# First level's steps at their own distances in chain slots, third norm of the isolated rows beside the fourth level, 31 dense slots beside the second level

## The reference

```
x = layernorm(x + L0(x))   # two-layer MLP, then a degree-normalised sum over edges and self loops
x = layernorm(x + L1(x))   # graph convolution with edge weights, relu, graph convolution
x = layernorm(x + L2(x))   # attention: leaky relu, z = h W, softmax of scores over the edges of a dst
x = layernorm(x + L3(x))   # messages from both ends and edge features, summed at dst, update MLP
# layernorm: (x - mean) / sqrt(var + 1e-5), no scale, no shift
```

## Time and profile before

| what | value |
|---|---|
| median of 3 runs (all) | 2968.99 us (2963.08, 2968.99, 2969.27) |
| profiled execution: own time, span | 2964.16 us, 2962.4 us |
| busy, share of the span: POOL, PE, DVE, ACT | 73%, 73%, 67%, 48% |
| mean granted TensorE clock | 0.852 |
| chain that ended last | POOL 54%, issue 20%, DVE 11%, PE 9%, DMA 3% |
| of it by line | POOL g_row L860 38%, x_with_info 8%, out_rows 7% |

### The profile page before, as it was taken

One profiled execution on the slowest core, in us unless ns is written; L12 is line 12 of the kernel. 1 busy time (PEld: TensorE's weight loads), 2 busy tenths in 40 slices (PEclk: granted clock), 3 DMA queues, 4 the chain that ended last, 5 costly groups with the idle time before them and its releaser, 6 DMA issues.

```text
span 2962.4 us, 39045 instructions
## 1 busy us (share of the span) xinstructions
PE 2167.5 (73%) x10332; PEld 1145.4 (39%) x10332; DVE 1987.5 (67%) x3848; ACT 1436.1 (48%) x2755; POOL 2174.0 (73%) x1666
## 2 busy tenths in 40 slices
PE   3998999959878646766577768998355576666665
PEld 1444444434444323434344434444255333333332
DVE  5665688858888747788599985777599433333332
ACT  2876677746545335565345446676222232233232
POOL 7888877778887258888588858888333688888887
PEclk9999999979989868897799979999655687777777
DMA  7998522223666366767354443443387322222221
GB/s 212 277 280 232 140 58 59 56 55 82 138 136 133 93 132 153 164 150 164 84 115 115 114 100 84 99 109 80 80 189 187 84 57 55 56 56 57 56 50 25
DMA packets 624034, 338.13 MB, mean 114 GB/s; under 512 B 536607, under 2 KB 585101, under 8 KB 623818
## 3 DMA queue, kind: packets, MB, share of 16 engines
q1 hardware_dynamic: 550217, 288.96, 38.8%
q0 software_dynamic: 73600, 46.68, 9.3%
HBM read 203.61 MB, written 130.80 MB: 113 GB/s over the span
## 4 chain that ended last, share of the span: by engine, by line
POOL 54%; issue 20%; DVE 11%; PE 9%; DMA 3%; SPq 2%; ACT 1%; DVEq 0%; POOLq 0%; ACTq 0%
POOL g_row L860 38%; POOL x_with_info L867 8%; POOL out_rows L867 7%; PE bank L1078 2%; PE bank L1101 2%; DVE rT L1696 1%; PE pair L987 1%; DMA g_row<-t_x,gidx 1%; DVE agg L1718 1%; PE bank L987 1%; PE pair L1058 1%; DVE x_r L1673 1%; DVE agg L1776 1%; DVE ss L1619 1%; PE pair L1069 1%
## 5 line engine op out<-in xcount | busy, mean ns | idle before, releaser
L860 POOL DMA_INDIRECT g_row<-t_x,gidx x600 | 814.0, 1357 | 263.6 <-issue 218.9
L1288 ACT ACTIVATE hid<-pair,b_up 128x1000 f32<-128x1000 f32 x375 | 406.1, 1083 | 45.9 <-PE pair L1059 44.2
L1079 PE MATMUL bank<-hid,w_dn 128*64 128x500 f32 x750 | 423.6, 648 | 0.0
L1078 PE MATMUL bank<-hid,w_dn 128*64 128x500 f32 x750 | 423.6, 648 | 0.0
L860 POOL DMA_INDIRECT g_row<-x_with_info,src_i x200 | 275.4, 1377 | 69.3 <-issue 56.7
L1058 PE MATMUL pair<-xT,w_top 64*128 64x500 f32 x550 | 314.6, 653 | 13.0 <-ACT hid L1288 10.5
L860 POOL DMA_INDIRECT g_row<-t_h,gidx x200 | 260.4, 1302 | 81.1 <-issue 80.8
L1059 PE MATMUL pair<-xT,w_bot 64*128 64x500 f32 x550 | 315.0, 654 | 0.0
L860 POOL DMA_INDIRECT g_row<-in_x,dst_i x200 | 260.2, 1301 | 68.0 <-issue 67.6
L1269 ACT ACTIVATE xT<-bank 128x500 f32<-128x500 f32 x275 | 160.3, 583 | 280.2 <-DVE rT L1696 163.2
L867 POOL DMA_INDIRECT out_rows<-n_r,fidx x200 | 251.2, 1256 | 60.9 <-issue 60.6
(11 more groups left out here) (257 smaller groups left out, 5157.9 us busy)
## 6 DMA issues: line engine op xcount, KB each, us to landing
x_in<-in_x_cols SPq DMA_DIRECT2D x100, 250.0 KB, 3.2
x_with_info<-wide SPq DMA_DIRECT2D x50, 476.0 KB
wide<-in_x SPq DMA_DIRECT2D x50, 448.0 KB
out_rows<-x_r SPq DMA_DIRECT2D x100, 224.0 KB
l_k<-keep_row SPq DMA_DIRECT2D x150, 125.0 KB
l_a<-t_x SPq DMA_DIRECT2D x150, 112.0 KB
l_k<-on_row SPq DMA_DIRECT2D x50, 250.0 KB
t_x<-x_r SPq DMA_DIRECT2D x100, 112.0 KB
```

The costliest lines, as they stand in the source:

```text
L860: return g.indirect_dma_start(out=to, out_offset=None, in_=table, in_offset=bass.IndirectOffsetOnAxis(ap=index[:, tile:tile + 1], axis=0), ...
L1078: T.matmul(run.down[0:D, 0:CH], w_dn[a.stage][:, 0:D], hid[a.b2][:, 0, :], start=True, stop=True)
L1079: T.matmul(run.down[D:128, 0:CH], w_dn[a.stage][:, 0:D], hid[a.b2][:, 1, :], start=True, stop=True)\
L1288: A.activation(hid[a.b2][:, :, :], run.up[a.b2][:, :, 0:CH], ACT.Relu, bias=b_up[:, a.stage:a.stage + 1]).then_inc(Cn["hid"], 1)
```

## The change

The steps of stage A are no longer hung on the arrival of the next isolated blocks. Each has its own distance, in chain slots, from the place of its block: `agg` 2 as before, `aggT` 3, `t1`, `t2` and `sq` 4, `ssum`, `std` and SP's load 5, `rows` 6, SP's store 7. No dense blocks stand among the isolated ones any more (`DENSE_MIXED` 3 to 0), and level B gets 31 places instead of 22. `third` moves as a whole from level B to level D, with its store one turn later and three more calls on SP after D's turns; the waits for its stores move with it, on DVE from the end of B to the end of D, ahead of the memsets.

```diff
-DENSE_MIXED = 3
-BESIDE_B, BESIDE_D, BESIDE_G = 22, 74, 0
+DENSE_MIXED = 0
+BESIDE_B, BESIDE_D, BESIDE_G = 31, 74, 0
...
-        def blocks_due(n):
-            return [a.b for a in ISO if a.place[0] + 2 == n] + [NI + i for i in range(5) if ISO[-1].place[0] + 3 + i == n]
-        def behind(b, lag):
-            b -= lag
-            return (b, b % 2, b % 4) if 0 <= b < NI else None
+        def block_at(n, slots):
+            found = [a.b for a in ISO if a.place[0] + slots == n]
+            return (found[0], found[0] % 2, found[0] % 4) if found else None
...
-            for step, at in (("rows", 4), ("st", 4), ("ld", 1), ("y", 0), ("sq", 1), ("ssum", 2), ("std", 3)):
+            for step, at in (("rows", 4), ("st", 5), ("ld", 1), ("y", 0), ("sq", 1), ("ssum", 2), ("std", 3)):
...
             with_a = sp_chain(WITH_A)
             for n in SLOTS_A:
-                for b in blocks_due(n):
-                    slot_a(b)
+                if c := block_at(n, 5):
+                    if c[0] + 4 < NI:
+                        ld_a(c[0] + 4)
+                if c := block_at(n, 7):
+                    st_a(c[0])
                 with_a(n)
...
 (SP, levels B and D)
-                  also=(...), each=third, run=WITH_B)
+                  also=(...), run=WITH_B)
-                  D_ld, [LD["lky2"]], D_st, LD["zc"], ..., behind=2, run=WITH_D, late=1)
+                  D_ld, [LD["lky2"]], D_st, LD["zc"], ..., behind=2, run=WITH_D, late=1, each=third)
+            for k in range(NC + 2, NC + 5):
+                third(k)
...
+            for r in range(2):
+                sp.wait_ge(third_st[r], 32 * len(range(r, NI, 2)))
...
 (PE)          aggT:  behind(b, 1)  ->  block_at(n, 3), after with_a(n)
 (ACT)         std:   behind(b, 3)  ->  block_at(n, 5);  sq: behind(b, 2) -> block_at(n, 4)
 (DVE, slot_a, between first(n) and rest(n), in this order)
               rstd:  behind(b, 4)  ->  block_at(n, 6)
               t1:    behind(b, 2)  ->  block_at(n, 4)
               ssum:  behind(b, 3)  ->  block_at(n, 5)
               rows:  behind(b, 4)  ->  block_at(n, 6)
               t2:    behind(b, 2)  ->  block_at(n, 4)
               agg:   behind(b, 0)  ->  block_at(n, 2)
...
 (ACT and DVE) each=third leaves shared_slots of WITH_B and joins that of WITH_D
-            shared_slots(slot_b, rest, WITH_B, 4, before=first, each=third)
-            for r in range(2):
-                dve.wait_ge([F["st0"], F["st1"]][r], 32 * len(range(r, NI, 2)))
+            shared_slots(slot_b, rest, WITH_B, 4, before=first)
...
-            shared_slots(slot_d, rest, WITH_D, 4, before=first)
+            shared_slots(slot_d, rest, WITH_D, 4, before=first, each=third)
+            for r in range(2):
+                dve.wait_ge([F["st0"], F["st1"]][r], 32 * len(range(r, NI, 2)))
```

More of the change, by code:

```diff
@@ L767, in _ @@
                   B_ld, [LB["xb"]], B_st, LB["rows"], lambda k, q: (rows_of(t2_d)[k], v4(n_r[q][:, :])), behind=3,
-                  also=(B_bst, LB["base"], lambda k, q: (chunks(base_d)[k], v4(l_src[q][:, :]))), each=third, run=WITH_B)
+                  also=(B_bst, LB["base"], lambda k, q: (chunks(base_d)[k], v4(l_src[q][:, :]))), run=WITH_B)
             all_stored(sp, B_st)
@@ L778, in _ @@
             level(lambda k, q: [(half(l_a[q]), rows_of(t3_d)[k])],
-                  D_ld, [LD["lky2"]], D_st, LD["zc"], lambda k, q: (z_d[k], zx[q % 2][:, :]), behind=2, run=WITH_D, late=1)
+                  D_ld, [LD["lky2"]], D_st, LD["zc"], lambda k, q: (z_d[k], zx[q % 2][:, :]), behind=2, run=WITH_D, late=1, each=third)
+            for k in range(NC + 2, NC + 5):
+                third(k)
             for r in range(2):
@@ L1104, in _ @@
             pe.wait_ge(Cn["rows"], normed_before(MAIN.hi))
-            def slot_a(b):
-                if c := behind(b, 1):
+            with_a = chain(WITH_A)
+            for n in SLOTS_A:
+                with_a(n)
+                if c := block_at(n, 3):
                     k, p, q = c
@@ L1114, in slot_a @@
                     mm.then_inc(LA["aggT"].sem, 1)
-            with_a = chain(WITH_A)
-            for n in SLOTS_A:
-                with_a(n)
-                for b in blocks_due(n):
-                    slot_a(b)
             pe.wait_ge(Cn["rows"], normed_before(WITH_A.hi))
@@ L1315, in _ @@
             HT2 = pair[1][:, 0, :]
-            def slot_a(b):
-                if c := behind(b, 3):
+            with_a = chain(WITH_A)
+            for n in SLOTS_A:
+                with_a(n)
+                if c := block_at(n, 5):
                     k, p, q = c
@@ L1322, in slot_a @@
                     root(a_sd[:, :], a_ss[:, :]).then_inc(LA["std"].sem, 1)
-                if c := behind(b, 2):
+                if c := block_at(n, 4):
                     k, p, q = c
@@ L1379, in _ @@
             act.wait_ge(s_idx, I_ALL)
-            shared_slots(slot_b, chain(WITH_B), WITH_B, 4, each=third)
+            shared_slots(slot_b, chain(WITH_B), WITH_B, 4)
             def after_c(at):
@@ L1410, in _ @@
             at_least(act, LC["rows"], NC)
-            shared_slots(slot_d, chain(WITH_D), WITH_D, 4)
+            shared_slots(slot_d, chain(WITH_D), WITH_D, 4, each=third)
             act.wait_ge(LD["c"], D_EXP)
@@ L1736, in block_scalar, with slot_a @@
                 return col.rearrange("p (s k) -> p s k", s=2).unsqueeze(3).to_broadcast([R, 2, TC, D])
-            def slot_a(b):
-                if c := behind(b, 4):
+            def slot_a(n):
+                if c := block_at(n, 6):
                     k, p, q = c
@@ L1767, in slot_a @@
                     V.tensor_tensor(a_w[p][:, :], a_v[:, :], a_base[q], ALU.add).then_inc(LA["t2"].sem, 1)
-                if c := behind(b, 0):
+                if c := block_at(n, 2):
                     k, p, q = c
@@ L1784, in _ @@
                 first(n)
-                for b in blocks_due(n):
-                    slot_a(b)
+                slot_a(n)
                 rest(n)
```

5 lines of the change are left out of this document (removed).

## The result

The changed kernel takes 2942.75 us (median of 4 runs, 2938.16 to 2945.02) against 2966.03 of the kernel before on the same chip (4 runs, 2960.08 to 2969.27): a ratio of 0.9916 with an interval of 0.9893 to 0.9939. The sign was right, the size was not.

The account below looks back on a forecast made before the run. POOL's gathers were taken to bound every stage touched. A -14, B -1, C 0, D +5 and D's end +3 gave -7 on the profiled 2964.16 us, so 2957, or 2959 with all four runs as one sample; range 2946 to 2972.

Parts of the forecast that it names:

- the third norm's part in B's slow gathers: Stage B: the third norm's leaving quickens the gathers by 4 us, within bounds of 0 to 23.
- a later last chunk: End of B: the chain runs until the last turns, so DVE may reach the last chunk later, +3 us (0 to 7).
- The `info` wait: Stage A: one POOL wait of 5.47 us instead of 0.30, for a late `info`, goes; last gather ends at 971.7.
- SP's lateness: Stage A: slow store issues make DVE wait 1 to 2 us in one pair of three; 3 us charged (0 to 20).
- The 4 us of slower gathers: Stage D: the third norm's instructions slow the gathers by 4 us (0 to 23), part of D's +5.
- End of D: +3: End of D: DVE's memsets wait for the last third-norm store, +2.8 us (1 to 5).
- Rival 1: A -17, B -8 + 3, D 0 to +1, end +3: -18 in all, 2948 us; chance 0.17.
- Rival 2: Stage D: third-norm instructions delay DVE, each of 25 double turns loses 0.5 us more; +5, 2971 us; chance 0.10.
- rival 3: Stage A: stores land 2 us late in every pair, 19 us of lateness instead of 3; +9, 2975 us; chance 0.11.
- Rival 4: Gathers stop for the full length of third-norm two-input instructions: B -20, D +36; +5 in all, 2971 us; chance 0.04.
- Seven instructions of 0.6 us: A's tail: DVE work that leaves the slots before SP's store waits, 4.4 us off the 66.7 from block 24's relu to B.
- the chances of the same time and of a slower one: Whole kernel: same within about 0.2% given 0.34, slower 0.15, faster 0.51, summed from forecast and rivals.

Follow-up runs that it names:

- e1: Changed kernel with three mixed dense blocks, 22 places beside B and the third norm in B as before, so own distances alone: 2952.23 us, ratio 0.9938.
- g3: Kernel before, with SP leaving a dense block's columns for a later slot instead of standing in a wait for them: 2944.41 us, ratio 0.992.
- e2: Kernel before, with only the third norm moved from B to D: 2956.89 us, ratio 0.9953.
- f1: Changed kernel with the old places (three mixed dense blocks, 22 places beside B); distances and third norm in D stay: 2937.8 us, ratio 0.9896.
- g2: g1 with the old places (three mixed dense blocks, 22 places beside B): 2917.33 us, ratio 0.9822.
- f4: Changed kernel, with SP leaving a dense block's columns for a later slot instead of standing in a wait for them: 2919.63 us, ratio 0.9836.
- f5: Changed kernel with the third norm's steps in D closer together, for its last store two turns earlier: 2937.33 us, ratio 0.9899.
- g1: Changed kernel with the changes of both f4 and f5: 2916.96 us, ratio 0.9833.
- h1: e2 plus 75 unused two-input VectorE instructions (125x512, both inputs in SBUF) in B: 2997.9 us, one run.
- h2: e2 plus 75 unused VectorE reductions of 125x512 from SBUF in B: 2961.9 us, one run.
- h4: e2 plus 75 unused VectorE float32 copies of 125x512, SBUF to SBUF, in B: 2972.94 us, one run.
- h3: Kernel before plus the 75 unused two-input VectorE instructions of h1, but in D: 2965.64 us, one run.
- e3: Kernel before with only the new places (no mixed dense blocks, 31 places beside B), third norm still in B: 2999.94 us, ratio 1.0099.
- e4: Changed kernel with the third norm left in B, so new places and own distances: 2993.24 us, ratio 1.0072.

## Why the prediction was wrong

It gave -7 us against a measured -26 of the two profiled executions; the 19 between lie as follows.

**B: the step that failed** is the price of the third norm's leaving. The prediction said of the third norm's part in B's slow gathers: "By its share of B's DVE work, 51.6 of 260.1 us, it is 4.6; I take 4", added 3 for a later last chunk, and came to -1. B gave 12.6, so these terms are 11.6 of the 19: 3.3 in the gathers (-4, measured -7.3), 8.3 in the tail (+3, measured -5.3). The small miss in the gathers is two that nearly cancel. Over the kernels that add no instructions or moves, B's gathers and tail together are 364.5, 364.6 and 363.2 us with the third norm and 22 places (before, e1, g3), 347.1, 351.9 and 344.0 without it (e2, f1, g2), and 351.9, 353.0, 349.4 and 353.3 with 31 places (after, f4, f5, g1). The third norm's leaving is worth 16, 12 of them in the gathers, where 4 stood in the sum; the nine units cost 4, nearly all in the gathers, where the sum had nothing. The bounds that the prediction set, 0 to 23, held; the choice within them, by share of busy time, was the error. A share supposes that every microsecond of DVE's work slows gathers alike. h1, h2 and h4 show that it depends on the operands (0.73, 0.20 and 0.58 us for each added microsecond), and h1 against h3 that it depends on the stage (37 us in B, 5 in D), by the rows above on what stands next to it.

The third norm's own 50 two-input instructions did not act as the added ones of h1 do, though. Counted in the same way in B of the kernel before, the 17 gathers that start inside one are 3.4 us longer than 1.27 each, the 18 that start up to 1 us ahead 0.6 us, and no gather of that stage is longer by more than 1.19. So they do not lengthen the level's run as the added ones do. In all 25 blocks a reciprocal (L1840) stands just ahead of the scaling (L1843), and in 23 the bias (L1832) follows behind it; that this keeps them apart from the run is argued, not shown. Some 10 of the 12 us are in gathers that start in the level's own `lxT`: these are 19.6, 15.7 and 12.5 us over with the third norm in B (before, e1, g3), 4.0, 9.4 and 4.4 without (e2, f1, g2). One of them in the kernel before, with DVE's instructions beside it:

```profile
1168.27 2.46 POOL L860 DMA_INDIRECT g_row<-t_x,gidx  x1 [0.30 <-issue]
...
1168.24 0.67 DVE L1812 TENSOR_TENSOR lxT<-agg,zx 64x500 f32<-64x500 f32 x1
1168.83 0.41 DVE L1819 TENSOR_TENSOR l_src<-w_r,l_b 125x256 f32<-125x256 f32 x1
1169.17 0.41 DVE L1825 TENSOR_TENSOR l_b<-l_a,b_row 125x256 f32<-125x256 f32 x1
1169.50 0.19 DVE L1643 RECIPROCAL rs_b<-sd_b 125x8 f32<-125x8 f32 x1
```

It ends at 1170.73, 1.15 us behind `l_b`, as the one of h1 ended 1.15 us behind the third added instruction. So the third norm slowed B mostly as the reductions of h2 did: by the moments at which gathers meet a run that is there anyway (28 start in `lxT` before, 14 in e2). The 4 of the sum is about what its own two-input instructions hold (4.0), by luck; the missing term is this shift, and what causes it stays open.

The +3 for the last chunk had the wrong sign. It rested on "DVE is as full as before", in which the 25 us of waits for PE that come with nine units were counted like work; by the same sum 51.6 us of work leave and 25 come. With less DVE work in all (238.7 us against 260.1), DVE reaches the last chunk earlier. Its last `m_r`, before and after, and one of the third norm's instructions in the tail before:

```profile
1411.01 0.41 DVE L1806 TENSOR_TENSOR m_r<-g_row,w_t 125x256 f32<-125x256 f32 x1
...
1384.37 0.43 DVE L1794 TENSOR_TENSOR m_r<-g_row,w_t 125x256 f32<-125x256 f32 x1 [0.25 <-DMA g_row<-t_x,gidx]
...
1417.51 0.69 DVE L1843 TENSOR_TENSOR wide<-wide,a_rs 125x512 f32<-125x512 f32 x1
```

The lag behind the end of the last gather (1406.35 and 1382.40) is 2.0 us instead of 4.7, half of the tail's 5.3. In the other half the third norm's instructions and stores no longer stand among those of the last chunks; what each is worth is not worked out.

**A: right in its steps, too cautious at the end (-14, measured -18.9).** The `info` wait went as worked out (gathers -5.3), block 24 came 9.3 us late where 11.0 was taken, and from its relu to B it is 62.5 where 66.7 - 4.4 = 62.3 was. SP's lateness was foreseen as one pair in three; seven waits of 0.4 to 2.4 us, 10 us in all, came. But the 3 us charged for them were not paid: POOL's pace hid all of it. The reading that less DVE work stands ahead of the tail's first wait, and that the two waits themselves stay, held (f4). What the prediction did not see is that the distances alone do it (e1: 74.0) and the places alone too (e3: 75.7). By ACT's timelines block 24 is 14.5 us late in e1 and 10.6 in e3, and from there to B it takes 59.5 and 65.1: the places take the lateness, as predicted, and the distances the rest, but the distances alone also take 4 us of the lateness and 7 of the rest.

**C:** 0 forecast, -1.8 measured, inside the scatter.

**D: +5, measured +1.0.** DVE had the room, as worked out: its waits for gathers fell from 50.9 to 6.5 us (some 10 were forecast) and POOL waited 0.3 us. The 4 us of slower gathers did not come: without the third norm D's gathers take 323.6, 323.0, 323.1, 320.6 and 321.3 us (before, e1, e3, e4, g3), with it 324.6, 322.4, 324.4, 323.4, 325.2, 326.2 and 322.9 (after, e2, f1, f4, f5, g1, g2), 1.9 us more in the mean.

**End of D: +3, measured +6.6.** The cause was right: the memsets wait for the third norm's last store. But DVE waits 5.50 us: SP issues the last two blocks' stores as one group of four that takes 2.31 us where 1.15 was taken, it ends at 2081.4, and the memsets start 2.8 us later, at 2084.19, where 1.9 was taken. Over these kernels the move costs 4.4 us here (39.3, 40.1, 40.7, 39.3 and 39.6 without, 45.9, 43.7, 43.3, 43.4, 43.4, 43.0 and 46.9 with).

**The rivals.** Rival 1 (A gives all, D asks nothing, -18) is what came, except that B gave more than twice what even it allowed (-12.6 for -5). Rival 2 (D becomes DVE's stage) and rival 3 (SP late in every pair) are refuted by the POOL idle of 0.3 us in D and by A's gathers. Rival 4 (gathers stand still for the two-input instructions) put +36 into D, and D gave 1. What it describes is seen in B of h1, but it is not the missed gain: the third norm's own two-input instructions held B's gathers 4 us in all. The Trainium skill, "SBUF — State Buffer", section "Who interferes with whom", lets a VectorE instruction with two SBUF inputs shut out a GpSimd instruction that reads SBUF, and so may a copy in a two-port mode; a reduction never does. The rows agree in kind: gathers are held beside the first (3.42 us for 1.27) and inside the copies of h4 (by up to 0.35 us), and those that start inside a reduction are not (0.09 us at most). They don't bear out a price of the instruction's length, as rival 4 took it: it is more than that in a run (h1's gather waited out five) and little in D (5 us for 51).

**Two sums of the prediction** don't come out as they stand. Seven instructions of 0.6 us are 4.2 us, not 4.4. By the parts that it names, the chances of the same time and of a slower one are 0.29 and 0.18, where 0.34 and 0.15 stand. Neither changes the forecast.

## What to carry to other kernels

Where POOL's indirect gathers pace a stage, do not price a DVE instruction that leaves or enters it by its share of DVE's time: look at which instructions stand back to back there, with two SBUF operands or as copies, and whether the moved ones lengthen such a run or only change when gathers meet it. Work that is free in one stage can cost several times as much in another that looks as full on the same counters. And in a stage's tail look for an in-order issue queue that stands in a wait: what is queued behind it can be worth as much (some 20 us here) as all else that is moved.

## What the runs showed of the hardware

The shortest indirect gather of 125 rows is 1.27 us in every stage and kernel here; the means of 1289 to 1539 ns come from some of the 200 that are held, up to 4.65 us in h1 (from its timeline). A gather that begins inside a two-input DVE instruction is mostly let go at about that instruction's end, although the next of its kind follows without a gap (held 0.52 us at most in D of h3); one that begins earlier in such a run may wait out all of it (2.0 to 2.7 us more in ten of those 21 in B of h1). What decides between the two is not in the records, and stays open.
